# A graph layer on one core: which destination tiles are multiplied densely, and how the others share their fetches

## The reference

```python
def _tagconv(x, src, dst, norm, W, b):
    out = x @ W[0]
    h = x
    for k in range(1, K + 1):
        msg = norm[:, None] * h[src]
        h = jax.ops.segment_sum(msg, dst, num_segments=x.shape[0])
        out = out + h @ W[k]
    return out + b
...
h = jax.nn.relu(_tagconv(x, src, dst, norm, W1, b1))
h = jax.nn.relu(_tagconv(h, src, dst, norm, W2, b2))
return _tagconv(h, src, dst, norm, W3, b3)
...
x = _layernorm(x + ref(x, ...), axis=-1)
```

## Time and profile before

| | before |
|---|---|
| runs, median (range) | 1311.15 us (1309.76 to 1312.9) |
| span of the profiled execution | 1308.7 us |
| runs' median less that span | 2.45 us |
| PE busy | 1262.6 us, 96% |
| DVE, ACT, POOL busy | 639.1, 361.3, 795.7 us |
| chain that ended last | PE 94%, line 976 alone 71% |
| line 976 | 4320 matmuls |
| line 686 | 801 fetches, 769.8 us busy |

### The profile page before, as it was taken

The page is one execution under the profiler, slowest core; times in us unless marked ns, Lnnn a source line. Parts: engine busy times, 40 slices in busy tenths (PEclk is TensorE's granted clock), DMA queues, the critical chain, the costliest instruction groups (busy, mean ns, idle before and its releaser), DMA issues.

```text
span 1308.7 us, 19260 instructions
## 1 busy us (share of the span) xinstructions
PE 1262.6 (96%) x7344; PEld 628.0 (48%) x7344; DVE 639.1 (49%) x1617; ACT 361.3 (28%) x863; POOL 795.7 (61%) x856
## 2 busy tenths in 40 slices
PE   3899999999999999999999999999999999999996
PEld 2555555444455554444444444554444444444442
DVE  7876663444445455434343335455443433344654
ACT  4766664221122222111221112222111111112221
POOL 5257663777466652777477646661677477747772
PEclk9999999999999999999999999999999999999998
DMA  3433332454234332444354423331344344425552
GB/s 101 151 100 112 103 107 68 138 145 129 82 105 114 110 104 64 132 130 134 94 148 129 129 75 114 113 110 52 111 133 130 90 125 131 128 84 152 156 155 69
DMA packets 86049, 149.10 MB, mean 114 GB/s; under 512 B 18670, under 2 KB 60128, under 8 KB 85950
## 3 DMA queue, kind: packets, MB, share of 16 engines
q0 software_dynamic: 38736, 105.79, 29.2%
q1 hardware_dynamic: 47214, 42.00, 9.9%
HBM read 115.70 MB, written 32.01 MB: 113 GB/s over the span
## 4 chain that ended last, share of the span: by engine, by line
PE 94%; DVE 3%; ACT 1%; DMA 1%; POOL 1%; issue 0%; SPq 0%; ACTq 0%; DVEq 0%; POOLq 0%
PE pb L976 71%; PE pb L887 9%; PE pb L889 5%; PE pb L910 3%; PE pb L822 2%; PE pb L981 2%; PE pb L934 1%; DMA xr<-in_x 0%; DVE pb L1315 0%; PE pb L915 0%; DVE V L1286 0%; DVE V L1083 0%; PE pb L875 0%; DMA gT<-in_table,idx 0%; ACT t L787 0%
## 5 line engine op out<-in xcount | busy, mean ns | idle before, releaser
L686 POOL DMA_INDIRECT GB<-vh,KS x801 | 769.8, 961 | 454.4 <-issue 230.7
L976 PE MATMUL pb<-V,A 128*128 128x512 f16 x4320 | 983.8, 379 | 0.0
L976 PEld LDWEIGHTS pb<-V,A 128*128 128x128 fp8e4 x4320 | 417.7, 98 | 464.9 <-issue 1.1
L1315 DVE SCALAR_TENSOR_TENSOR pb<-pb,cst,t 128x256 f32<-128x256 f32 (+1 forms) x225 | 109.9, 489 | 365.8 <-ACT t L787 365.6
L787 ACT ACTIVATE t<-pb,cst 128x256 f32<-128x256 f32 (+1 forms) x250 | 118.1, 473 | 503.1 <-PE pb L981 473.1
L887 PE MATMUL pb<-Whl,gT 128*128 128x512 f16 x576 | 203.9, 382 | 6.8 <-DVE gT L1264 3.4
L889 PE MATMUL pb<-Whl,gT 128*128 128x256 f16 x576 | 157.5, 274 | 0.0
L1286 DVE SCALAR_TENSOR_TENSOR V<-V,pb 128x256 f16<-128x256 f16 (+1 forms) x225 | 94.2, 420 | 92.1 <-ACT V L761 90.7
L761 ACT ACTIVATE V<-pb 128x256 f16<-128x256 f32 (+1 forms) x225 | 85.6, 382 | 134.7 <-DVE pb L1315 134.3
L887 PEld LDWEIGHTS pb<-Whl,gT 128*128 128x128 f16 x576 | 56.4, 98 | 82.2 <-issue 21.1
L1191 DVE TENSOR_REDUCE stat<-V 128x1 f32<-128x256 f16 x225 | 91.4, 412 | 0.3
(11 more groups left out here) (161 smaller groups left out, 453.3 us busy)
## 6 DMA issues: line engine op xcount, KB each, us to landing
vh<-V SPq DMA_DIRECT2D x216, 128.0 KB
GB<-vh,KS POOLq DMA_INDIRECT x801, 2.8
xr<-in_x SPq DMA_DIRECT2D x48, 128.0 KB, 2.9
out<-g SPq DMA_DIRECT2D x24, 128.0 KB, 1.9
xr<-in_W SPq DMA_DIRECT2D x16, 128.0 KB, 2.2
V<-in_W SPq DMA_DIRECT2D x2, 512.0 KB, 4.4
vh<-V SPq DMA_DIRECT2D x18, 26.5 KB
bb<-in_b SPq DMA_DIRECT2D x3, 128.0 KB, 5.1
```

What stands on the lines that cost most here:

```text
L686: pool.indirect_dma_start(GB[:, slot, :], None, vh[vbuf[(L, k + 1)]][:, :], bass.IndirectOffsetOnAxis(ap=KS[:, p:p + 1], axis=0))\
L976: mm = pe.matmul(acc[:, :], A8[:, a, t * P:(t + 1) * P], src[:, a, :], start=False, stop=(n == NT - 1), skip_group_check=True)
L1315: dve.scalar_tensor_tensor(hi, hi, cst[0:r, 1, t:t + 1], lt, ALU.mult, ALU.add).then_inc(S["s_d1"], 1)
```

## The change

Dense tiles become 0 to 18 and tile 24; the gathered ones are 19 to 23. Tile 24 is treated as 64 columns of a second matrix AT in 16 bits; its two halves are two chains of matmuls of 256 columns on two 128x64 tiles of the array. The gathered tiles have 20 groups, two neighbouring groups form a pair with nine fetches (four windows of its own for each, and a fifth window that ends the first group and serves the second too), 90 fetches a hop. A fifth step therefore has four matmuls on two slots. The positions of the steps change. Row numbers and limits of the 121 windows are now worked out by a table of rules: POOL fills the table, PE and ACT bring it onto partitions, POOL does the arithmetic in a chain.

```diff
-TD = 20
+TD = 19
 ND = TD * P
+DENSE = [*range(TD), NT - 1]
+BH = GS * -(-ND // GW)
+NTB = -(-N // GD) - BT
+NW = BH + NTB
+PG = 2
+PW = PG * GV
+PF = PW - 1
+NHOP = 2 * (NT - 1 - TD)
+NGA = NHOP * PF
-FIRST = {3: 2, 5: 5, 7: 7, 9: 10, 11: 12, 13: 15, 15: 17, 17: 19, 18: 20, 19: 25}
-STEPS = {5: 5, 9: 10, 13: 15, 17: 20, 19: 25}
+FIRST = {3: 2, 5: 5, 7: 7, 9: 10, 11: 12, 13: 15, 15: 17, 17: 20, 18: 22, 19: 25}
+STEPS = {5: 5, 9: 10, 12: 15, 15: 20, 19: 25}
...
+def window(g, v):
+    return g * GV + (v if g % PG == 0 else (v + 1) % GV)
...
 def fetches(s):
-    t, v = s // GV, s % GV
-    g = P // GH * t
-    d = g * GV + v * min(P // GH, GN - g)
-    return [(d + j, (g + j) * GV + v) for j in range(min(P // GH, GN - g)) if (g + j) * GV + v < NGA]
+    v, g = s % GV, P // GH * (s // GV)
+    d = PF * (g // PG) + P // GH * v
+    if v < GV - 1:
+        return [(d + j, window(g + j, v)) for j in range(P // GH)]
+    return [(d + j, window(g + PG * j, v)) for j in range(P // (GH * PG))]
+
+def multiplied(s):
+    v, g = s % GV, P // GH * (s // GV)
+    share = PG if last_step(s) else 1
+    d = PF * (g // PG) + P // GH * v
+    return [(d + j // share, window(g + j, v)) for j in range(P // GH)]
...
 @@ schedule @@
-            for i in range(TD):
-                out.append(("P", L, k, i))
+            for i, t in enumerate(DENSE):
+                out.append(("P", L, k, t))
...
+        AT = sb("AT", [P, NT, TC + HALF], F16)
...
 @@ gpsimd, before it scales x @@
+            pool.memset(rules, 0.0).then_inc(S["s_pc"], 1)
...
-            pool.wait_ge(S["s_i5"], 2)
-            pool.indirect_dma_start(G[0:GP, QW, :, :].rearrange("p s e -> p (s e)"), None, table[:, :],
-                                    bass.IndirectOffsetOnAxis(ap=idx[0:GP, QW:QW + 1], axis=0)).then_inc(s_gl[QW], 16)
+            for j, many in enumerate((1.0, float(FULL), 1.0, 1.0)):
+                pool.memset(less[:, NPAIR * j:NPAIR * (j + 1)], -many).then_inc(S["s_pc"], 1)
...
+            pool.iota(place, pattern=[[1, P]], base=0, **iota).then_inc(S["s_pc"], 1)
+            pool.wait_ge(S["s_pc"], RULED + 1)
+            pool.wait_ge(S["s_cp5"], 3)
+            done5(pool.tensor_scalar(vals[:, :], per[:, 12:16], 0.0, 0.0, ALU.max, ALU.add))
...
+            done5(pool.tensor_copy(idx[0:NR, QW:QW + 1], two[:, 4:5]))
+            pool.indirect_dma_start(G[0:NR, QW, :, :].rearrange("p s e -> p (s e)"), None, table[:, :],
+                                    bass.IndirectOffsetOnAxis(ap=idx[0:NR, QW:QW + 1], axis=0)).then_inc(s_gl[QW], 16)
+            done5(pool.tensor_scalar(per[:, 11:12], per[:, 11:12], float(JZ), 0.0, ALU.add, ALU.add))
...
+            done5(pool.tensor_scalar(place, place, OUTSIDE, per[:, 11:12], ALU.mult, ALU.subtract))
+            pool.wait_ge(S["s_ki"], QK // KQ)
+            pool.wait_ge(s_gl[QW], 16)
+            pool.tensor_copy(wf[0:NR, 0:P], G[0:NR, QW, 0, :]).then_inc(S["s_k5"], 1)
+            done5(pool.tensor_copy(wf[0:NR, P:2 * P], G[0:NR, QW, 1, :]))
+            pool.tensor_tensor(wf[0:NR, P:2 * P], wf[0:NR, P:2 * P], place, ALU.add).then_inc(S["s_k5"], 1)
...
 @@ tensor, start @@
+            pe.wait_ge(S["s_pc"], RULED)
+            pe.matmul(bank[1][0:4 * NPAIR, 0:1], less, ones16[0:1, 0:1], start=False, stop=True,
+                      skip_group_check=True).then_inc(S["s_gc"], 1)
+            for d in range(12):
+                mm = pe.matmul(bank[0][0:NR, d:d + 1], rules[:, d, :], ones16[0:1, 0:1], start=True, stop=True,
+                               skip_group_check=True)
+            pe.wait_ge(S["s_cp5"], 1)
+            for j in range(4):
+                mm = pe.matmul(bank[2][0:NR, j:j + 1], mine[:, j, :], found[:, :], start=True, stop=True,
+                               skip_group_check=True)
...
 @@ tensor, gather @@
-                for j, (d, p) in enumerate(fetches(st)):
+                for j, (d, p) in enumerate(multiplied(st)):
...
 @@ tensor, work: tile 24 @@
+                mm = tail(L, k, acc) if t == NT - 1 else project(L, k, t, acc)
+                if k < 3 and t == NT - 1:
+                    src = V[vbuf[(L, k + 1)]]
+                    for a in range(NT - 1):
+                        pe.matmul(acc[0:HALF, 0:F], AT[:, a, TC:TC + HALF], src[:, a, 0:F], start=False, stop=False,
+                                  skip_group_check=True)
+                        pe.matmul(acc[HALF:P, 0:F], AT[:, a, TC:TC + HALF], src[:, a, F:512], start=False,
+                                  stop=(a == NT - 2), skip_group_check=True)
+                    mm = pe.matmul(acc[0:HALF, 0:F], AT[:, NT - 1, TC:TC + HALF], src[:, NT - 1, 0:F], start=False,
+                                   stop=True, skip_group_check=True)
...
 @@ vector @@
-            def fetched():
-
-                dve.wait_ge(s_gl[QW], 16)
-                dl_(dve.tensor_copy(wf[0:GP, 0:P], G[0:GP, QW, 0, :]))
...
+            def tail_keys():
+
+                s_, d_ = KS[:, NE:NR], KD[:, NE:NR]
...
+                link(dve.tensor_scalar(ai, s_, 7, None, ALU.logical_shift_right))
...
+                link(dve.tensor_scalar(KKb[:, BH:NW], dl, MID - VALID, None, ALU.add))
```

More of the change, by code:

```diff
@@ L359, in spot, with groups_of @@
     return n % RB if n < NT - 4 else RB + n - (NT - 4) if n < NT - 2 else n - (NT - 2)
-def groups_of(t):
-    last = [-1] + [min(NG - 1, (P * (i + 1) - 1) // GW) for i in range(TD)]
-    return list(range(last[t] + 1, last[t + 1] + 1)) if t < TD else []
+def groups_of(i):
+    last = [-1] + [(P * (j + 1) - 1) // GW for j in range(TD)] + [NG - 1]
+    return list(range(last[i] + 1, last[i + 1] + 1)) if i < len(DENSE) else []
 def trailing(sched, empty, split):
@@ L390, in trailing @@
         if (L, k) == (0, 2):
-            if t < TD:
-                gs = [("B", gi) for gi in groups_of(t + 1)]
-                out += gs[:empty] + waiting + gs[empty:split] + ends() + gs[split:] + [("A", t)]
+            if t in DENSE:
+                gs = [("B", gi) for gi in groups_of(DENSE.index(t) + 1)]
+                out += gs[:empty] + waiting + gs[empty:split] + ends() + gs[split:] + [("A", DENSE.index(t))]
                 waiting = []
@@ L511, in bass_tag_gnn_layernorm @@
             few = (L, k) == (0, 2) or (L, k) == (0, 3) and t >= NT - 4
-            if (L, k, t) == (0, 2, 0) or k < 3 and t >= TD:
+            if (L, k, t) == (0, 2, 0) or k < 3 and t not in DENSE:
                 b = 7
@@ new lines, in _ @@
+            pool.iota(rules[:, 11, NE:NR], pattern=[[GD, NTB]], base=BT * GD - JZ, **iota).then_inc(S["s_pc"], 1)
+            pool.memset(mine, 0.0).then_inc(S["s_pc"], 1)
+            pool.wait_ge(S["s_pc"], RULED - 4)
+            for j in range(3):
+                pool.affine_select(out=mine[:, j, 0:NE].rearrange("p (u m) -> p u m", m=PW),
+                                   in_=mine[:, j, 0:NE].rearrange("p (u m) -> p u m", m=PW),
+                                   compare_op=ALU.not_equal, fill=1.0, base=-NPAIR * j,
+                                   pattern=[[-1, NPAIR], [0, PW]], channel_multiplier=1).then_inc(S["s_pc"], 1)
@@ L908, in gather @@
                     pe.wait_ge(s_gb[slot], 16 * use)
-                    if t < NT - 1:
-                        mm = pe.matmul(acc[GH * j:GH * j + GH, :], SG[:, p, :], GB[:, slot, :], start=False,
-                                       stop=last_step(st), skip_group_check=True)
-                        continue
-                    for half in range(2):
-                        at = HALF * half + GH * j
-                        mm = pe.matmul(acc[at:at + GH, 0:F], SG[:, p, :], GB[:, slot, F * half:F * half + F],
-                                       start=False, stop=last_step(st), skip_group_check=True)
+                    mm = pe.matmul(acc[GH * j:GH * j + GH, :], SG[:, p, :], GB[:, slot, :], start=False,
+                                   stop=last_step(st), skip_group_check=True)
                 mm.then_inc(S["s_ps" if last_step(st) else "s_gm"], 1)
@@ L939, in work @@
                 e = pe_no[(L, k, t)]
-                if k < 3 and t >= TD:
+                if k < 3 and t not in DENSE:
                     reckon(L, k, t)
@@ L1389 @@
     vd = [nc.dram_tensor(f"vd{i}", (NP, F), _mybir.dt.float32, kind="Internal").ap() for i in range(2)]
[L1390 removed]
+    vh = [nc.dram_tensor(f"vh{i}", (TAILAT + HALF, 2 * F), _mybir.dt.float16, kind="Internal").ap() for i in range(2)]
     bass_tag_gnn_layernorm(nc, ap["x"], ap["table"], ap["heads"], ap["edges"], [ap["W1"], ap["W2"], ap["W3"]],
```

210 lines of the change are left out of this document (134 added, 76 removed).

## The result

The changed kernel takes 1302.81 us, the median of four runs (1302.17 to 1303.39); the kernel before takes 1311.74 beside it. The ratio is 0.9935, with a 95% interval of 0.9921 to 0.9950: faster by 0.65%. The forecast was 1301.1 with a range of 1294 to 1309. The profiled execution took 1303.25 us. Its span is 1301.5, against 1308.7 before: 7.2 us less, where the prediction's terms gave 10.0.

What follows compares the result with a forecast made beforehand. PE's matmuls, one after the other, were taken to bound the kernel (PE busy 96%). The terms summed to -10.0 us against the 1308.7 us span: 1298.7, or 1301.1 with 2.45 us to the runs' median; range 1294 to 1309.

Steps and rivals of the forecast that it cites:

- eight hops on PE: Hops 1 to 8: PE's removed tiles less the added ones gain 1.92 us a hop, -15.4 us in all.
- clock behind hop 0: Behind hop 0's end: PE, idle in a wait of 5 us, loses granted clock, +1.5 us.
- thin fetches: Hops 1 to 8: +0.5 us in all for hops where the fetches' cover doesn't reach; ends 0 and 6 us.
- hop 0: With only 16 slots, twelve fetches are left late, PE waits at the hop's end: 2.4 us longer than before.
- start: Setup before the first layer: POOL's new chain delays the scaling of x, +1.5 us, between 0 and 6.
- end: Last tile's norm: the last two tiles end 1.93 us apart instead of 1.30, so the last waits less, -0.5 us.
- The pair at 0.11 us: Tile 24's dense half: two chains run side by side, 0.11 us a pair, making the half 3.40 us.
- serial rival: Dense half: pairs run one after the other, 0.22 us each, half 5.9 us, total around 1320 us; chance 0.11.
- slow ones among the twelve: End of hop 0: slow fetches among the last twelve add 0.4 us, or 2.8 us if all are slow.
- The cover of the fetches: Hops 1 to 8: tile 22's last fetch lands at 101.9, PE wants it at 102.7; about 1 us to spare.
- second rival: Fetches become the bound, a microsecond lost in each of six hops, 1307 us; chance 0.17, shared with a long start.
- brings POOL to about 29.5: Setup: POOL's chain ends and scaling of x starts near 29.5 instead of 27.69; 1.5 us delay taken.

Runs made afterwards that it cites:

- e7: Changed kernel with all 24 upper-half matmuls of the dense half ahead of the 24 lower-half ones: 1314.98 us, ratio 1.0022 to the kernel before.
- e10: Changed kernel with the dense half's matmuls in blocks, four upper then four lower, six times; on a slow-clock chip: 1766.24 us, ratio 0.9737 to the kernel before.
- e3: Changed kernel with most of hop 0's later gathered steps placed earlier (FIRST only): 1296.62 us, ratio 0.9880 to the kernel before.
- e5: Changed kernel with POOL delayed by three or seven scratch operations before tile 22's fetches in hops 1 to 8: 1308.08 us (three), 1320.64 us (seven).
- e4: Changed kernel with the edits of e2 and e3 together: 1290.61 us, ratio 0.9842 to the kernel before.
- e11: Changed kernel with the kernel before's places for gathered tiles in hops 1 to 8: 1349.72 us, ratio 1.0289 to the kernel before.
- e2: e1 plus the second half of POOL's chain moved into gaps behind scalings 1 to 4 of x: 1297.28 us, ratio 0.9887 to the kernel before.
- e1: Changed kernel with the five small memsets moved ahead of POOL's fills and chain: 1297.32 us, ratio 0.9890 to the kernel before.
- e6: Kernel before with the change's places for gathered tiles in hops 1 to 8, nothing else: 1365.88 us, ratio 1.0412 to the kernel before.
- e8: Changed kernel with the edits of e1 and e3, POOL's chain left whole; on a slow-clock chip: 1756.52 us, ratio 0.9681 to the kernel before.
- e9: First run of e11's kernel, on a chip where the kernel before took 1813 us: 1816.88 us, ratio 1.0007 to the kernel before.

## Why the prediction was right, and where it was not

Term by term, in us of the span:

| term | predicted | measured |
|---|---|---|
| eight hops on PE | -15.4 | -16.2 (8 x -2.02) |
| layer boundaries (hops 2, 3, 5, 6) | none | -3.6 |
| clock behind hop 0 | +1.5 | +2.3 |
| clock lost before in hop 6, not after | none | -1.2 |
| thin fetches | +0.5 | +0.7 (one wait of 0.32, in hop 3) |
| hop 0 | +2.4 | +2.4 |
| start | +1.5 | +8.1 |
| end | -0.5 | +0.2 |
| sum | -10.0 | -7.2 |

The terms of the last column are rounded. The clock term of hop 6 is what hop 6 took more than hop 3 before (133.66 for 132.47), the thin fetch what hop 3 took more than hop 6 after (129.76 for 129.04), and the end what the last hop changed (-1.84) less a plain hop's -2.02.

- **The pair at 0.11 us: right, shown.** The dense half is 3.27 us for 3.40. e7 and e10 say why: two matmuls on different halves run side by side wherever they are within some four of each other. The serial rival fell. (Its dense half of 5.9 us should have been 3.40 and 24 x 0.11, 6.0.) The Trainium skill (TensorEngine Tiling (Array Packing), Feature Incompatibilities) excludes the fast weight load here; the trace shows loads that hide within 0.11 us of a lone matmul of 64 columns, so whatever load it was, it cost nothing.
- **Hop 0: right, shown.** 2.4 us longer, a stall of 5 us, twelve fetches from 215.77. e3 takes away both the stall and the clock behind it, 5.05 and 2.3 us. The prediction gave 0.4 us for slow ones among the twelve; all eleven distances between them are 1.25. That says nothing on the Trainium skill's "DVE blocks DMA" trap (SBUF — State Buffer): DVE's last one-hot operation starts at 212.64 and lasts 0.67, and the first of the twelve fetches is at 215.77. Earlier in hop 0 fetches and one-hots do meet, and there the fetches are slower. Of the changed kernel's 90, 59 overlap a one-hot operation by over 0.1 us. They take 1.11 us in the median, 33 of them over 1.0. The other 31 take 0.95, one of them over 1.0. The kernel before shows the same (62 at 1.10, 28 at 0.95). No run tries what holds them up.
- **The cover of the fetches: right, shown.** 102.7 against 101.9 was the forecast, 0.8 us; the trace gives 0.5 to 0.6, e5 0.5 to 0.8. The second rival was less than one microsecond away. The 0.7 us that were lost came from none of these places but from the one fetch of hop 3 that was used 4.72 us behind its start. e3 and e4 have a wait in the same hop too (0.49 and 0.77 us), e7 hasn't; why that fetch is late wasn't tried. But the places stood on narrower ground than the text told: it priced the new ones and never asked what the old would cost. e11 answers, 47 us.
- **The start: wrong.** The step that failed is "brings POOL to about 29.5": the term was 1.5 and measured 8.1. The chain itself was longer. It began at 22.93 for 22, the first eight operations took 4.14 us with their waits for 2.4, the seven behind the fetch 3.79 for 2.45, and it ended at 33.1. That has little weight, at most 1.7 us (e2). The weight is in what the sum left out altogether: the five memsets, which the change moves behind that chain, and the two engines that queue behind the last of them. ScalarE's Sqrt waited 6.72 us, DVE's RECIPROCAL behind it 6.77. e1 prices them at 5.5 by the medians and 3.9 in the trace. The prediction followed POOL from its chain to the scaling and asked only what waits for the scaling; it did not ask who waits for each instruction that the chain is now ahead of. A third part, 1.4 to 2.5 us, is in neither edit (hop 0's first tile ends at 73.76 in e4 and 74.86 in e2, for 72.40 before); what it is wasn't tried.
- **The boundaries and hop 6: not foreseen.** Before the change PE stood 0.33 and 1.52 us ahead of projections at 498.01 and 500.36; after, 0.21 at 507.47. That is 1.64 us less at each of the two boundaries. The four hops around them give 3.6 us more than the others, so these waits are most of it. The prediction took PE for busy through a whole hop and subtracted its matmuls; the idle time at the boundary was in none of its terms. In e6 the same waits are down from 1.85 to 0.96 us with nothing changed but the places, so about half of the gain is theirs. The rest came with the dense half and the new order of the last tiles, and no run parts these. The 1.2 us of hop 6 are a clock that the profiled execution before lost and the one after did not: luck of the two executions.
- **The end: wrong by 0.7.** DVE's two last tiles still come 1.6 us apart (1288.85 and 1290.47), since ScalarE reached the half only at 1288.27.

So the time was right by luck: an error of +6.6 at the start (and +0.7 at the end) met one of -4.6 in the hops, -18.0 for -13.4 with their clock and fetches. A reader should take the mechanism from this prediction and not its closeness.

## What to carry to other kernels

When a chain is put into an engine's queue, list every instruction that now stands behind it, however small, and for each the engine that waits for it; a memset of 0.1 us cost 5 us here, and moving it back is free. When transfers are taken from a ring of slots, the places of their users and the number of fetches between them are one design: work them out together, hop by hop and for the hop with the fewest slots by itself. A stall of lone matmuls costs more than its waits add up to (5.05 us for 3.04 here), and some clock behind it.

## What was not expected of the hardware

- Matmuls on two halves of the array need not alternate: four and four run side by side in full (3.27 us), and in e7 the lower half's first one started at 355.83, ahead of three earlier in the program (355.93, 356.04, 356.15). The Trainium skill (TensorE: Matmul & The Clock Gate, Part 3) says "MATMULs are pc-monotone in start AND end — strict FIFO, no reordering"; the trace disagrees for the starts. Of the 0.6 us that the dense half of e7 saves (5.27 for 3.27 + 2.64), four matmuls that run beside the other half where the blocks meet are 0.44.
- On one chip the kernel before took 1813 us, with an average granted clock of 0.86 to 0.87 in every execution. The traces taken there (e8, e9, e10) have 265 to 293 gaps of PE, 272 to 308 us in all and up to 3.8 us long, in which it waits for nothing that the profile shows; the changed kernel's trace has none. They show a clock that swings between 0.5 and 1.00. What makes the gaps isn't known. The change with e1 and e3 gave 3.2% there (e8, 0.9681), where e4, which has e2's edit besides, gave 1.6% at the usual clock.
